# Convolution taps of three of eight tiles moved from VectorE to GpSimd, and gate products moved to the head of the mixing block

## What is computed

```python
xz   = x @ in_proj_w.T                     # x part: 8 tiles of 128 channels, gate part: 8 tiles
conv = causal_dwconv(x_part, conv_w, 4 taps) + conv_b
u    = silu(conv)                          # feeds dt, B and C of the scan
...
y    = scan(u, dt, A, B, C) + D * u
out  = (y * silu(gate_part)) @ out_proj_w.T
```

## Time and profile before

| | us |
|---|---|
| median of 3 runs (lowest, highest) | 3955.61 (3954.16, 3958.93) |
| the profiled execution's own time | 3953.2 |
| its span, first to last instruction | 3951.4 |
| TensorE busy | 3507.1 (89%) |
| VectorE busy | 3177.0 (80%) |
| ScalarE busy | 1607.1 (41%) |
| GpSimd busy | 1339.6 (34%) |

### The profile page before, as it was taken

The page is one execution under the profiler, slowest core; times in us unless marked ns, Lnnn a source line. Parts: engine busy times, 40 slices in busy tenths (PEclk is TensorE's granted clock), DMA queues, the critical chain, the costliest instruction groups (busy, mean ns, idle before and its releaser), DMA issues. The chain is left out here.

```text
span 3951.4 us, 41155 instructions
## 1 busy us (share of the span) xinstructions
PE 3507.1 (89%) x15310; PEld 1468.3 (37%) x15310; DVE 3177.0 (80%) x2733; ACT 1607.1 (41%) x2189; POOL 1339.6 (34%) x493
## 2 busy tenths in 40 slices
PE   5777779998999979998999989988999989976998
PEld 1222243334333443334333443334333443323444
DVE  5999569787999869887999869897999869895333
ACT  5666343214655353214655343214655343212001
POOL 3454304352344304352344304352344304351000
PEclk9788899989899999989899989999999989987999
DMA  6678402122233402122233302122233302110322
GB/s 230 244 277 299 172 15 74 58 74 71 88 106 97 136 22 72 60 72 72 88 105 98 131 27 72 57 75 72 88 105 98 133 25 72 58 45 11 104 96 72
DMA packets 105429, 382.92 MB, mean 97 GB/s; under 512 B 14224, under 2 KB 27920, under 8 KB 102800
## 3 DMA queue, kind: packets, MB, share of 16 engines
q1 hardware_dynamic: 85792, 346.50, 25.5%
q10 hardware_dynamic: 19440, 33.79, 3.1%
HBM read 290.80 MB, written 64.32 MB: 90 GB/s over the span
## 5 line engine op out<-in xcount | busy, mean ns | idle before, releaser
L300 PE MATMUL ps<-r,ring 128*128 128x512 bf16 (+1 forms) x2040 | 782.6, 384 | 0.0
L297 PE MATMUL ps<-xr,ring 128*128 128x512 bf16 x1568 | 613.1, 391 | 0.3 <-PEq L1822 0.3
L301 PE MATMUL ps<-xr,ring 128*128 128x512 bf16 x1568 | 610.6, 389 | 0.0
L297 PE MATMUL ps<-r,ring 128*128 128x512 bf16 (+3 forms) x1384 | 547.8, 397 | 55.2 <-DVE xc L1107 17.8
L301 PE MATMUL ps<-r,ring 128*128 128x512 bf16 (+3 forms) x1384 | 546.9, 396 | 0.0
L1159 POOL TENSOR_TENSOR hh<-hh,bc 128x2048 f32<-128x2048 f32 x72 | 334.7, 4649 | 520.9 <-DVE hh L1069 520.9
L1159 POOL TENSOR_TENSOR bc<-bc 128x2048 f32<-128x2048 f32 x64 | 304.2, 4752 | 344.7 <-DVE bc L1069 344.7
L1159 POOL TENSOR_TENSOR r<-r,bc 128x2048 f32<-128x2048 f32 x56 | 260.9, 4659 | 298.5 <-DVE r L1069 298.5
L1069 DVE TENSOR_TENSOR_SCAN hh<-da,hh 128x2048 f32<-128x2048 f32 x72 | 325.6, 4522 | 1.2
L1110 DVE TENSOR_TENSOR xc<-xc,ps 128x512 f32<-128x512 f32 x176 | 119.3, 678 | 225.0 <-PE ps L301 225.0
L1069 DVE TENSOR_TENSOR_SCAN bc<-da,bc 128x2048 f32<-128x2048 f32 x64 | 296.1, 4627 | 0.5
(11 more groups left out here) (269 smaller groups left out, 6519.5 us busy)
## 6 DMA issues: line engine op xcount, KB each, us to landing
ring<-wsplit SPq DMA_DIRECT2D x216, 768.0 KB, 4.2
r<-wstream SPq DMA_DIRECT2D x54, 768.0 KB, 6.9
ring<-wsplit SPq DMA_DIRECT2D x76, 512.0 KB, 4.0
wsplit<-ring SPq DMA_DIRECT2D x38, 768.0 KB, 4.5
...
```

Source lines behind the costliest of these rows:

```text
L297: mm = pe.matmul(out, w_hi, x_hi, start=start, stop=False)
L300: pe.matmul(out, w_hi, x_lo, start=False, stop=False)
L301: return pe.matmul(out, w_lo, x_hi, start=False, stop=stop)
```

## The change

Three things change, all of them only for sequences with a successor, but for the last item:

1. In `close_batch` the taps of tiles 2, 4 and 6 are computed by GpSimd (`other_taps_by_pool`), each tap as a tensor_scalar (multiply into a scratch row `scaled_x`) and a tensor_tensor (add), with a semaphore wait between; VectorE keeps tiles 0, 1, 3, 5 and 7.
2. The five gate tiles leave `close_batch`, where fillers (18 and 26 matmuls) take their place, as they already did in the last sequence. In `mix_batch` gates 0, 1 and 2 are computed at the head (0 and 1 ahead of the first products in place of the 12 fillers, 2 behind them), and gates 3 to 7 in the scan loop.
3. The load of the next x and its split move from `mix_batch` to the norm block ahead of it, and weight slot `W_PROJ + 3` is loaded first. In the scan loop the list `work` is given out evenly over the eight steps, in the last sequence too.

```diff
@@ ScanInputs
     def silu(self, act, j):
-        act.wait_ge(self.conv, 3 * (j + 1))
+        earlier = sum(i in self.pool_taps for i in range(j))
+        if j in self.pool_taps:
+            act.wait_ge(self.pconv, 3 * (earlier + 1))
+        else:
+            act.wait_ge(self.conv, 3 * (j - earlier + 1))
...
+    def other_taps_by_pool(self, pool, j):
+        v, x = self.v(j), self.source(j)
+        earlier = sum(i in self.pool_taps for i in range(j))
+        pool.wait_ge(self.tap, j + 1)
+        for n, c in enumerate((2, 1, 0)):
+            late = 3 - c
+            if n:
+                pool.wait_ge(self.pconv, 3 * earlier + n)
+            scaled = self.k.scaled_x[:, 0:T - late]
+            pool.tensor_scalar(scaled, x[:, 0:T - late], self.cw[:, 4 * j + c:4 * j + c + 1], None, ALU.mult).then_inc(self.pscaled, 1)
+            pool.wait_ge(self.pscaled, 3 * earlier + n + 1)
+            pool.tensor_tensor(v[:, late:T], v[:, late:T], scaled, ALU.add).then_inc(self.pconv, 1)
@@ layer_norm
+        @blk.gpsimd
+        def _(pool):
+            if split is not None:
+                pool.wait_ge(loaded, 16)
+                for c in range(KM):
+                    low(pool, split[:, c, :], load[0][:, c, :])
@@ mix_batch, TensorE
+            if ahead:
+                first_gate(0)
+                first_gate(1)
+            else:
+                keep_busy(k, pe, 2, 12)
             wt = k.w.wait(pe, W_MIX)
-            keep_busy(k, pe, 2, 12)
...
+            if ahead:
+                first_gate(2)
+                k.w.done()
             pe.wait_ge(zdone, 2)
             pe.wait_ge(zsplit, 1)
             mixes(0)
...
-            work = [(value, 2), (value, 3)] + [(gate, o) for o in range(4)] + ([(ahead_product, n) for n in range(J0 + 3)] if ahead else [])
+            work = [(value, 2), (value, 3)] + [(gate, o) for o in range(4)] + ([(ahead_product, n) for n in range(2 * J0) if not J0 <= n < J0 + 3] if ahead else [])
...
-                until = min(3 + 2 * g + g // 4, len(work))
+                until = max(len(work) * (g + 1) // G, min(3, len(work)))
@@ mix_batch, ScalarE
+            def first_silu(j):
+                act.wait_ge(first_mm, j + 1)
+                act.activation(k.bc[:, 6144 + j * T:6144 + (j + 1) * T], bank(j), ACT.Silu).then_inc(first_in, 1)
+                act.wait_ge(first_in, j + 1)
+                act.dma_start(k.gates_dram[:, j, :], k.bc[:, 6144 + j * T:6144 + (j + 1) * T]).then_inc(first_stored, 16)
...
-                for j in range(3):
-                    n = N0 + J0 + j
+                for j in range(3, J0):
+                    n = N0 + J0 + j - 3
...
-                act.wait_ge(stored, 3 * 16)
+                for i in range(4):
+                    act.wait_ge(stored[i], 32 if i == 3 else 16)
+                act.wait_ge(first_stored, 3 * 16)
@@ mix_batch, GpSimd
-                if ahead and g < 2:
-                    for c in range(2 * g, 2 * g + 2):
-                        low(pool, k.xn_lo[:, c, :], k.xn[:, c, :]).then_inc(nsplit, 1)
@@ close_batch, TensorE
-            if ahead:
-                gate(3)
-                gate(4)
-            else:
-                keep_busy(k, pe, 0, 18)
+            keep_busy(k, pe, 0, 18)
...
-            if ahead:
-                pe.wait_ge(cent, KM)
-                for j in range(5, J0):
-                    gate(j)
-                pe.wait_ge(gate_in, 5)
-            else:
-                keep_busy(k, pe, 0, 26)
+            keep_busy(k, pe, 0, 26)
@@ close_batch, ScalarE
             if ahead:
-                for j in range(3, J0):
-                    act.wait_ge(gate_mm, j - 2)
-                    act.activation(k.dt0[:, j, :], gate_bank(j), ACT.Silu).then_inc(gate_in, 1)
                 s.silu(act, 2)
@@ close_batch, GpSimd
             if ahead:
                 s.build_spread(pool)
+                s.other_taps_by_pool(pool, 2)
                 for j in range(3):
                     s.split_x(pool, j)
             for c in range(KM):
                 split_out(c)
             if ahead:
-                for j in range(3, J0):
+                s.other_taps_by_pool(pool, 4)
+                s.split_x(pool, 3)
+                s.other_taps_by_pool(pool, 6)
+                for j in range(4, J0):
                     s.split_x(pool, j)
@@ close_batch, VectorE
-            if ahead:
-                s.other_taps(dve, 2)
             dve.wait_ge(rs, 1)
...
-                for j in range(3, 6):
-                    s.other_taps(dve, j)
+                s.other_taps(dve, 3)
+                s.other_taps(dve, 5)
...
-                s.other_taps(dve, 6)
                 s.other_taps(dve, 7)
```

94 lines of the change are left out of this document (46 added, 48 removed).

## The result

The changed kernel takes 3973.97 us (median of 5 runs, 3973.19 to 3981.82), the kernel before beside it 3958.02 (5 runs, 3954.16 to 3959.19): 16 us **slower** by the medians, and a ratio of 1.0047 with a 95% interval of 1.0035 to 1.0059. I had forecast 12 us faster (3944, from a median of 3955.6), and the time lies above the range too.

The account below looks back on a forecast made before the run. TensorE bounds the projections, VectorE the scan loop; GpSimd's late splits delay the closing block. 1.9 + 0.2 + 1.9 - 8.0 = -4.0 us, three times -12.0, from 3955.6 to 3943.6, said as 3944; range 3933 to 3968.

Parts of the forecast that it names:

- Closing block, what is added on GpSimd: Closing block: each tap on GpSimd is a multiply, taken at 0.7 us, and an add, taken at 1.1 us.
- P: GpSimd's time for one tile of taps in the closing block: 5.8 us, bounds 5.0 and 9.2.
- rival (b): Closing block: GpSimd becomes the bound, `low_product(4)` waiting for tile 4's split; slower, 3969 at P = 9.2; 0.17 with (d).
- (d): Closing block: no effect, something else holds up the product by Wo; +4.0 a sequence remains, 3968; 0.17 with rival (b).
- 932.9 + 3P: Closing block: when GpSimd's split of tile 4 is done once tile 2 also delays `split_out`; 960.5 at P = 9.2.
- Contention: GpSimd and VectorE side by side: VectorE's taps take 1.25 us each beside GpSimd's splits against 0.77.
- The closing block without the taps: Closing block, gates gone: earlier norm factor, `silu(2)` and `split_out`; product by Wo ends 8.3 us earlier, taken as -8.0.
- Head of the mixing block: Mixing block's start: gates 0 and 1 cost nothing, gate 2 costs +1.9 us, passed on in full; bounds 0 and +2.6.
- End of it: Scan loop's last step: three gate tiles instead of one, the last gate's store ending late; +1.9 us, bounds +0.8 and +3.5.
- Norm block: Norm block ahead of the mixing block: the x load and splits moved there cost +0.2 us, bounds 0 and +1.
- Last sequence: Last sequence: only the list is given out differently, beside a VectorE-bound loop; 0.
- What bounds the kernel now: Opening step: which engine sets the pace; closing block's gates hold up the mixing output, GpSimd waiting 14.74 us for `silu(2)`.

Follow-up runs that it names:

- e12: e9 with all three tiles of GpSimd's taps behind the splits of the mixer's output, and the low-rank products of tiles 2 to 6 behind the variances: 3974.91 us.
- e3: The changed kernel with each tap's multiply on GpSimd as a tensor_tensor against the broadcast weight column instead of a tensor_scalar: 3956.61 us.
- e9: The changed kernel with the low-rank product of tile 4 behind the norm's variances on TensorE instead of ahead of them: 3953.79 us.
- e8: The changed kernel with each of GpSimd's multiplies by a tap's weight issued twice: 4012.38 us.
- e1: The changed kernel with all taps of the closing block back on VectorE in the order of before; gates stay moved: 3942.86 us.
- e7: e1 with the scan loop's list given out earlier, so that two gates and not three stand in the last step: 3939.49 us.
- e2: The kernel before with only the taps of tiles 2, 4 and 6 on GpSimd; the gates stay: 3969.72 us.
- e4: The kernel before with only GpSimd's splits of the mixer's output moved ahead of its split of tile 2, which waits for `silu(2)`: 3928.33 us.

## Why the prediction was wrong

1. **The step that failed is the price of the multiply on GpSimd**, in "Closing block, what is added on GpSimd": 0.7 us taken, 1.78 measured (1.57 at the least, 2.41 at the most). I had bounded it from above by the tensor_tensor, 1.04 to 1.46, and the least that was measured lies above that bound. P was 9.1 to 9.6 us, not 5.8, at my upper bound of 9.2 or past it. It is 8.6 even with VectorE idle (e12), past the 7.8 from which I had let rival (b) begin. The reasoning under it ("with one input it is nearest the copy") was an assumption on how the engine's cost follows from the number of inputs, and no row showed it. e3 refutes it: with two inputs the multiply is 0.6 us cheaper.

   The Trainium skill ("GPSIMD Engine Reference", section "When to use GPSIMD") calls the engine roughly line rate for one input. For tensor_scalar on f32 the trace says otherwise: 1.57 us is over three times the 0.43 that I had estimated from it. The Trainium skill's advice there, to leave elementwise work to VectorE, is borne out: a tile of taps is 9.1 to 9.6 us on GpSimd and 2.31 on VectorE. For one operation with two inputs the rows show less than the factor of two that the Trainium skill gives there, 1.04 us against 0.69 (before, 931.12); the 0.77 that I had set beside it is a whole tap.

2. **What followed is rival (b)**, at the place that I had named. It decides from P = 7.8, and P was beyond it: `low_product(4)` waited for the split of tile 4, and the variances behind it came 3.3 us later than before. My formula, 932.9 + 3P, gives 0.9 at P = 9.4. The rest are two things of 1.2 us each that it lacks. The three splits of x ahead of `split_out` took 4.4 us instead of some 3.1, and the product of tile 4, after the wait, took 975.25 - 972.73 = 2.5 us at a granted clock of 0.50 where I had 1.3. I had also written that from there on every wait is on ScalarE, TensorE and VectorE. e9 shows one more on GpSimd: `silu(6)` stands ahead of ScalarE's eviction of the variances. That the rival's 3969 is only 5 from the 3974 measured owes something to luck: of the 28.4 us between the profiles it has the mixing blocks about right (12 of 13.1), but the closing blocks at 1 instead of 9.0, most of it in the third. e9 shows the mechanism (6.2 us at the variances and 15 us in the closing blocks for the place of one product), e8 its slope. I had given it 0.17 with (d), too little when half of P hung on an operation that no row held; its two bounds were both extrapolations, and one measured row of tensor_scalar would have decided the case.

3. *Contention* I had named as evidence for (b), and left out of the sum. VectorE's two-input steps take 1.52 us beside GpSimd and 0.69 alone (in e12, at 929.65), its taps up to 1.35 against 0.77. The rule of the Trainium skill ("GPSIMD Engine Reference", section "Key points") that the two share SBUF interfaces when VectorE has two SBUF inputs agrees with these rows. Its part in the time was not tried by itself; for GpSimd e12 bounds it at 1 us a tile.

4. *The closing block without the taps*: right in the first sequence, too large in the others. Forecast 8.0 earlier at the product's end, e1 shows 7.4, 5.8 and 4.1; its closing blocks are 15 us shorter in all, not 24. The means, silu(2) and `split_out` of the first came where I had put them. I had read one sequence and, but for 0.3 us, counted it three times.

5. *Head of the mixing block*: forecast +1.9, measured +2.7 at the first addition, of which gate 2 is 2.0 and gates 0 and 1, put at nothing, 0.7 (a gate tile takes 2.7 us, not the 2.6 of my sum). *End of it*: forecast +1.9, measured +2.4, and e7 shows that it is the last gates' place. But "passed on in full" holds only where the projections run at the lower clock: in the changed kernel the first scan read comes 64.7, 64.7 and 61.5 us into the block, before 62.0, 62.0 and 61.1, and in e1 at 61.5 to 61.6 every time. Where the clock was 0.89 the head's cost had been all but regained by then. So the two sizes were 0.8 and 0.5 too small, and the blocks' lengths still grew by 13.1 us where I had 11.4: less than 2 us of the miss.

6. *Norm block* (+0.2): the stretch that holds it takes 214.2 or 217.3 us before and after alike, so no cost is seen. *Last sequence* (0): 207.7 before, 211.4 after; but e2, which leaves the list there as it was, has 211.4 too, and e9 and e3, with the new list, 204.3. The list is not the cause; what is stays open.

7. I judged in "What bounds the kernel now" that the gates held the output up in a roundabout way, through `silu(2)`. That was right, and a closer look at my own sentence would have shown that no gate has to move for it: the order of five instructions on GpSimd is enough (e4).
